# Layer 2 of a two-layer network: the scan's decays move from four PSUM banks to three places in SBUF, and the banks become work banks

## What is computed

```
def _branch(x, ...):                       # once forward, once over the reversed positions
    xc = silu(causal_conv4(x))             # 384 inner channels
    dt, Bc, Cc = ...                       # from xc @ W_xproj.T ; dt = softplus(... @ W_dt.T + bias)
    A = -exp(A_log)                        # [384, 16]
    for t in positions:                    # state h[384, 16]
        h = h * exp(dt[t] * A) + (dt[t] * xc[t]) * Bc[t]
        y[t] = sum_n h[:, n] * Cc[t, n]
    return y + xc * D
out = ((y_f + y_b) * silu(z)) @ W_out.T + b_out
```

## Time and profile before

| | |
|---|---|
| median of 3 runs | 19136.82 us (19125.12 to 19158.0) |
| profiled execution | 19135.61 us; its trace spans 19133.8 us |
| mean granted TensorE clock | 0.885 |
| busy share PE, DVE, ACT, POOL | 80%, 90%, 69%, 88% |
| layer 2, first scan to last scan, image 1 | 257 to 1217 us |
| from there to the first scan of image 2 | 234 us |

### The profile page before, as it was taken

The page is one execution under the profiler, slowest core; times in us unless marked ns, Lnnn a source line. Parts: engine busy times, 40 slices in busy tenths (PEclk is TensorE's granted clock), DMA queues, the critical chain, the costliest instruction groups (busy, mean ns, idle before and its releaser), DMA issues. The chain is left out here.

```text
span 19133.8 us, 189246 instructions
## 1 busy us (share of the span) xinstructions
PE 15370.5 (80%) x45152; PEld 5349.5 (28%) x45152; DVE 17219.0 (90%) x13583; ACT 13164.2 (69%) x33157; POOL 16897.2 (88%) x11028
## 2 busy tenths in 40 slices
PE   7888878878888788887888778887788878888778
PEld 2222222222222222222222222222222222222222
DVE  7989989899898998989989899898998989989899
ACT  6767767677676776767767677676776767767676
POOL 6979979799797997979979799797997979979799
PEclk8888888888888898888888888888888988888888
DMA  2424424244242442424424244242442424424244
GB/s 73 120 61 112 119 66 118 59 113 118 68 117 60 113 117 68 117 62 115 113 68 118 65 114 109 68 120 65 113 109 68 120 66 114 107 68 120 68 116 104
DMA packets 880283, 1820.18 MB, mean 95 GB/s; under 512 B 189530, under 2 KB 594804, under 8 KB 879028
## 3 DMA queue, kind: packets, MB, share of 16 engines
q1 hardware_dynamic: 879028, 1806.77, 37.6%
HBM read 1083.46 MB, written 245.63 MB: 69 GB/s over the span
## 5 line engine op out<-in xcount | busy, mean ns | idle before, releaser
L1159 DVE TENSOR_TENSOR_SCAN arena<-ps,arena 128x897 f32<-128x897 f32 x5376 | 10985.9, 2064 | 477.9 <-ACT arena L1311 225.4
L1363 POOL TENSOR_TENSOR arena<-arena 128x896 f32<-128x896 f32 x5376 | 9417.5, 1770 | 225.5 <-DVE arena L1159 210.1
L1294 ACT ACTIVATE ps<-arena,A 128x448 f32<-128x448 f32 x10752 | 6390.8, 627 | 2400.0 <-DVE arena L1159 2318.3
L1065 PE MATMUL ps<-arena,rep 128*64 128x448 f32 x21504 | 5506.2, 642 | 1605.0 <-POOL arena L1363 1596.4
L1355 POOL TENSOR_TENSOR arena<-arena 128x896 f32<-128x896 f32 x2688 | 4772.4, 1775 | 210.0 <-DMA arena<-arena 137.5
L1065 PEld LDWEIGHTS ps<-arena,rep 128*64 128x64 f32 x21504 | 1483.1, 154 | 5247.2 <-POOL arena L1363 2835.9
L1148 DVE TENSOR_TENSOR arena<-ps,arena 128x896 f32<-128x896 f32 x2688 | 2862.7, 1065 | 75.4 <-PE ps L985 59.8
L1018 PE MATMUL ps<-arena,diag 128*128 128x448 f32 x5248 | 2193.6, 562 | 77.1 <-DVE arena L1122 77.1
L1057 PE MATMUL ps<-arena,skipd 128*128 128x448 f32 x1344 | 797.0, 679 | 711.6 <-DVE arena L1135 588.3
L1018 PEld LDWEIGHTS ps<-arena,diag 128*128 128x128 f32 x5248 | 985.3, 195 | 1265.5 <-issue 1041.7
L1344 POOL TENSOR_TENSOR arena<-arena 128x448 f32<-128x448 f32 x672 | 656.9, 982 | 512.8 <-DVE arena L1128 512.8
(11 more groups left out here) (171 smaller groups left out, 18878.1 us busy)
## 6 DMA issues: line engine op xcount, KB each, us to landing
arena<-bc_rows SPq DMA_DIRECT2D x3584, 224.0 KB, 4.6
arena<-arena SPq DMA_DIRECT2D x4160, 112.0 KB, 3.6
x_projected<-arena SPq DMA_DIRECT2D x112, 672.0 KB, 3.6
y_forward<-arena SPq DMA_DIRECT2D x112, 672.0 KB, 5.6
arena<-x_projected SPq DMA_DIRECT2D x112, 672.0 KB, 4.8
arena<-y_forward SPq DMA_DIRECT2D x112, 672.0 KB, 6.2
x<-in_x SPq DMA_DIRECT2D x119, 336.0 KB, 3.6
x_normed<-arena SPq DMA_DIRECT2D x112, 336.0 KB, 5.1
```

Source lines behind the costliest of these rows:

```text
L1065: m = e.matmul(ps[64 * h:64 * h + 64, YBANK, 0:T], rep[:, 0:64], pr[:, (q - 1 + h) % NPR, a * T:a * T + T], start=False, stop=p == NP - 1 ...
L1159: e.tensor_tensor_scan(rev(hh[:, q % NH, 0:W2], s), rev(decays(q)[:, 0:W2], s), rev(bb[:, q % NB, 0:W2], s), car[:, 2 * k + p % 2, n:n + 1 ...
L1294: e.activation(two(decays(q))[:, a, :], dt2[:, r % NR2, p % 2, :], ACT.Exp, scale=Am[s][:, 2 * k + p % 2, n:n + 1]).then_inc(c_ex, 1)
L1363: e.tensor_tensor(pr[:, q % NPR, :].rearrange("p (a b) -> p a b", a=2), two(hh[:, q % NH, :]), cr[:, p - p % 2:p - p % 2 + 2, :], ALU.mult ...
```

## The change

`DECAY` goes. A new SBUF array `ee` has `ND = 3` places of 2 x 449 values, and `decays(q)` is place `q % 3` of it, so ACT writes the decays to SBUF and the scan reads both of its streams from SBUF. ACT waits for scan `q - 3` in place of scan `q - 2`. PSUM banks 0 to 3 join banks 6 and 7 as work banks of the side chains over the whole image, and the wait of the first two units for the early chains goes.

```diff
@@ -38,8 +38,9 @@
 AHEAD, LAG = 2, 2
 NB, NH, NPR = 3, 3, 4
 NXC, NDT, NDU, NR2 = 5, 3, 3, 3
-
-DECAY, DUBANK, YBANK, WBANK = (0, 2), 4, 5, (6, 7)
+ND = 3
+
+DUBANK, YBANK, WBANK = 4, 5, (6, 7, 0, 1, 2, 3)
 
 
 class Waits:
@@ -152,15 +153,13 @@
     read = {(name, i, e): t for p in plans[1:4] for t, name, i, e in p}
     release = {(name, i, e): read.get((last.get(name), i, e)) for _, name, i, e in plans[0]}
     for k, (t, name, i, e) in enumerate(a for a in plans[0] if a[1] != "dp"):
-        banks = WBANK if t >= -10 else [*WBANK, 0, 1, 2, 3]
+        banks = WBANK
         b = banks[k % len(banks)] if t < -10 else min(banks, key=lambda n: until.get(n, -99))
         until[b] = release[name, i, e]
         jobs[name, i, e] = (k, b, used.get(b, 0))
         used[b] = used.get(b, 0) + 1
-        if t < -10:
-            first = dict(used)
     jobs["cv", 0, 0] = (None, DUBANK, 0)
-    return plans, jobs, first
+    return plans, jobs
 
 
 class Steps:
@@ -881,6 +880,7 @@
     res = take(T)
     br = take(NP, T, phase=2)
     cr = take(NP, T, phase=2)
+    ee = take(ND, 2 * T1)
     bb = take(NB, 2 * T1)
     hh = take(NH, 2 * T1 + 2, phase=0)[:, :, 0:2 * T1]
     pr = take(NPR, 2 * T)
@@ -891,7 +891,7 @@
     car = take(2 * EJ, NP)
     tmp = gz[0:CP, :, :]
 
-    plans, jobs, first = side_schedule()
+    plans, jobs = side_schedule()
     plan_pe, plan_act, plan_dve, plan_pool, plan_sp = plans
 
     n1 = Norm("c", (5, 6))
@@ -936,8 +936,7 @@
         return ap.rearrange("p (a b) -> p a b", a=2)[:, :, 0:T]
 
     def decays(q):
-        b = DECAY[q % 2]
-        return ps[:, b:b + 2, :].rearrange("p a b -> p (a b)")[:, 0:2 * T1]
+        return ee[:, q % ND, :]
 
     def b_loaded(w, i, p):
 
@@ -1076,8 +1075,8 @@
         e.tensor_scalar(nrm[:, 0, T:2 * T], x1[:, 1, ch(0)], gs[:, 4, 1:2], gs[:, 5, 1:2], ALU.mult,
                         ALU.add).then_inc(c_ns, 1)
         e.memset(xh[0][:, :, 0:3], 0.0).then_inc(c_pad, 1)
-        for b in DECAY:
-            e.memset(ps[:, b, T:T1], 0.0)
+        for n in range(ND):
+            e.memset(ee[:, n, T:T1], 0.0)
         steps = Steps(plan_dve)
 
         def side(g):
@@ -1285,10 +1284,7 @@
         def decay(q):
             r, i, k, p, s = pair(q)
             spread(w, s_dt, 2 * (r % NR2) + p % 2, r)
-            if q < 2:
-                for b in range(4):
-                    w.wait_ge(c_wf[b], first.get(b, 0))
-            w.wait_ge(c_sc, q - 1)
+            w.wait_ge(c_sc, q - ND + 1)
             for a in range(2):
                 n = p - p % 2 + a
                 e.activation(two(decays(q))[:, a, :], dt2[:, r % NR2, p % 2, :], ACT.Exp,
```

## The result

The kernel after takes 28,041.79 us (median of 4 runs, 28,027.57 to 28,045.21) against 19,143.94 before (median of 4 runs, one more than in the table above): a ratio of 1.4647, 95% interval 1.4622 to 1.4673. The forecast was 28,300, in a range of 27,300 to 29,400.

The account below looks back on a forecast made before the run. The prediction took POOL to bound layer 2's stage, at 5.175 us a round. Turns with scans make it 8.65; 168 rounds less 11 us idle add 573 us an image, 9,170 in all: 19,135.6 to 28,300 us, range 27,300 to 29,400.

Parts of the forecast that it names:

- the exclusion: A DVE instruction with two SBUF streams and a POOL instruction run one after the other; applies to all 5376 scans.
- The prices of a turn: Layer 2: scan behind POOL 1.89 us, POOL instruction behind a scan 1.57, POOL behind POOL 1.725.
- The order: Layer 2 rounds go scan, POOL, scan, POOL, POOL, taking 8.65 us in place of 5.175.
- Two scans in a row: Rival: DVE keeps its turn, so scan, scan, POOL, POOL, POOL; 8.94 us a round, 29,080 us; chance 0.10.
- rival of whole instructions in turn: Rival: nothing of the later instruction is hidden; 9.44 us a round, 30,420 us; chance 0.07.
- The sum: 168 rounds an image add 584 us, less 11 of idle time: 573; sixteen images 9,170, giving 28,300 us.
- the idle time: POOL's 21 us idle per image in layer 2's stretch; half was let stay, taking 11 us off.
- The third place and the banks: Three decay places with a looser ACT wait: worth nothing; four more work banks: nothing, up to 25 us an image.
- ACT's write to SBUF: ACT writing decays to SBUF, not PSUM: no difference taken; at 0.05 us each, 34 us an image, hidden.
- the half that I gave: PE's busy share falls to about half and its clock may fall; even at 1.2 GHz its work fits, so nothing.
- What the profile was to show: Layer 2: POOL's and DVE's busy shares both near 100%, because a waiting instruction counts as busy; rounds of 8.65 us.

Follow-up runs that it names:

- only-memory kernel: Kernel before with only the decays' memory changed: two places in SBUF, ACT's wait and the two work banks as before; 28,064.54 us, ratio 1.4654.
- kernel with one stream back in PSUM: Kernel after, with the scan reading zeros from PSUM and decays from SBUF, four work banks 6, 7, 2, 3, recurrence not computed; 19,204.28 us, ratio 1.0026.
- memset kernel: Kernel after, with POOL's output replaced by a memset of the same 896 values, so h times C isn't computed; 22,192.04 us in one run.

## Why the prediction was right

- **The mechanism.** Right: the exclusion read from layer 1's 448-value instructions holds for layer 2's 896-value ones, with both streams full. The only-memory kernel shows that the move to SBUF is the whole cause, the kernel with one stream back in PSUM that two SBUF streams are the condition, and the memset kernel that POOL has to read.
- **The prices of a turn.** From record ends of scans and POOL instructions in the trace after, medians: a scan behind POOL 1.885 us (5,328 of them; forecast 1.89), a large POOL instruction behind a scan 1.56 (5,120; 1.57), one behind another 1.72 (2,944; 1.725). With two scans and three POOL instructions this is 8.61 us; the round is 8.62, the forecast 8.65.
- **The order.** Right: scan, POOL, scan, POOL, POOL. Two scans in a row came up 48 times in 5,376, three an image. The rival of whole instructions in turn is out by the same rows: 1.885 and not 2.06, 1.56 and not 1.77.
- **The sum.** The stretch was forecast at 1,533 us and is 1,515. Sixteen times 18 us are 290; between images it got 1.5 us longer, fifteen times, and what is left is about the gap between 28,300 and 28,042. When each turn is counted from the record end of the one before, the scans take 635 us of an image's stretch, POOL's large instructions 812 and its small ones 67, which fills the 1,515. The sum had 635, 817 and 70 for them, and 10 us of idle time on top. So the term that was most mis-sized is the idle time, which I had only guessed: POOL does stand idle 10 us of the stretch, but all but half a microsecond of it while a scan runs, so it adds nothing to the turns.
- **What was to be worth nothing.** The third place and the banks: no gain, as said. ACT's write to SBUF: 0.656 us in place of 0.627, which with overlaps is 143 us of ACT's busy time over all images (6,533.4 for 6,390.8), hidden since ACT is busy 708 of 1,515 us. TensorE: its granted clock in the stretch fell to 0.73, its busy time rose to 942 us, so its share is 62% and not the half that I gave, still well under the stretch.
- **What the profile was to show.** POOL is near 100% in the stretch (1,505 of 1,515 us), DVE is not (88%). I said that both wait inside instructions; but the even scans wait for POOL's product at a semaphore, outside, 0.67 us a round (the median), as the order that I had worked out implies. The odd scans wait outside too, 0.41 us on the mean.

## What to carry to other kernels

Before moving an operand of a DVE instruction from PSUM to SBUF, count the SBUF streams that it then reads: with two, and POOL reading SBUF all the time, their times add up: POOL at 97% and DVE at 95% of 960 us became turns that fill 1,515. Look for an instruction elsewhere in the same trace that already has the new form, and compare its shortest and longest record: here a scan of half the size in the other layer gave the price of a turn within 1%. And a shorter turn is no gain by itself: with layer 1's keys in PSUM the turns shrank and DVE's idle time grew by more.

## What was not expected of the hardware

- A POOL memset into SBUF of 896 values takes 0.84 us and was never stretched beside a DVE instruction with two SBUF streams (5,376 memsets, 0.852 us at most), while a POOL product of that size beside one is stretched from 1.77 to as much as 3.67.
- In layer 2 the engine that waits gets the next turn: 1,184 scans of the kernel after were issued right behind another with a POOL instruction waiting, and POOL went in between every time. That is no rule for all: with L614 moved behind L592, POOL was waiting at the end of L592 in 72 cases, and in 22 of them the DVE instruction behind it (L599) went first. One of the 22, DVE and then POOL, whose product of 0.98 us waits for both; what decides was not followed:

```profile
2578.11 1.13 DVE L592 TENSOR_TENSOR_SCAN arena<-wuv,arena 128x448 f32<-128x448 f32 x1
2579.16 0.60 DVE L599 SCALAR_TENSOR_TENSOR arena<-arena 128x448 f32<-128x448 f32 x1
...
2578.14 2.46 POOL L838 TENSOR_TENSOR arena<-arena 128x448 f32<-128x448 f32 x1
```
- TensorE's granted clock in the stretch of scans fell from 0.89 to 0.73 of full speed (2.4 GHz), a mean over parts at that level and at 1.2 GHz, when TensorE's busy share there fell from 80% to 62%: it ran the same instructions over 1.58 times the time. Its matmuls at L1064 (L1065 before) went from 0.642 to 0.791 us on the mean.
